# Starting the next stage inside the stage before it, at four seams of a one-core kernel

## What is computed

```python
x = x + L0_conv(_ln_c(x)); t = tokens(x); t = t + L0_ffn(_ln_t(t))   # 13x13 + 3x3 depthwise; experts
x = x + L1_conv(_ln_c(x)); t = tokens(x); t = t + L1_ffn(_ln_t(t))   # attention, 6 heads; experts
x = x + L2_conv(_ln_c(x)); t = tokens(x); t = t + L2_ffn(_ln_t(t))   # deformable attention; experts
x = x + L3_conv(_ln_c(x)); t = tokens(x); t = t + L3_ffn(_ln_t(t))   # linear attention; binarised layer

def _L1_ffn_ref(x, gate_w, gate_b, w1, b1, w2, b2):                  # the same for L0 and L2
    probs = softmax(einsum('bsd,de->bse', x, gate_w) + gate_b)       # 4 experts, the best 2 kept
    masked = probs * mask; masked = masked / (sum(masked) + 1e-09)
    h = gelu(einsum('bsd,edh->ebsh', x, w1) + b1)                    # 96 -> 384
    y = einsum('ebsh,ehd->ebsd', h, w2) + b2
    return einsum('bse,ebsd->bsd', masked, y)
```

## Time and profile before

| | |
|---|---|
| time, median of 3 runs | 1336.79 us (1335.22 to 1337.23) |
| the profiled execution | 1334.63 us, its span 1332.8 us |
| PE busy | 1177.9 us, 88% of the span |
| PE weight loads | 1020.5 us, 77% |
| DVE busy | 809.8 us, 61% |
| ACT busy | 487.3 us, 37% |
| POOL busy | 249.9 us, 19% |
| mean granted clock of TensorE | 0.929 of full speed |

### The profile page before, as it was taken

How to read it: one execution, slowest core, us unless ns; L and a number is a source line. 1 busy time by engine, 2 the same in 40 slices (tenths; PEclk the granted TensorE clock), 3 DMA queues, 4 the chain that set the end, 5 groups by cost and what they waited for, 6 DMA issues and landing times. The chain is left out here.

```text
span 1332.8 us, 23847 instructions
## 1 busy us (share of the span) xinstructions
PE 1177.9 (88%) x8368; PEld 1020.5 (77%) x8368; DVE 809.8 (61%) x2938; ACT 487.3 (37%) x948; POOL 249.9 (19%) x232
## 2 busy tenths in 40 slices
PE   2979999948999997999996999997999968998776
PEld 2978888937999996888894767676889867886455
DVE  6137676555666653767656665545767667776556
ACT  3524333314554543433331223224333322232542
POOL 3002212121010100221213343322121212111200
PEclk9989999967999998999996999997999988999577
DMA  3201010010000000000000000000000000000000
GB/s 136 76 24 49 14 47 0 0 48 1 1 2 1 2 1 1 1 1 0 0 1 0 1 1 2 1 1 1 1 1 0 0 1 1 1 1 1 3 10 36
DMA packets 11561, 15.67 MB, mean 12 GB/s; under 512 B 7385, under 2 KB 9007, under 8 KB 11346
## 3 DMA queue, kind: packets, MB, share of 16 engines
q1 hardware_dynamic: 10754, 12.86, 3.0%
q10 hardware_dynamic: 720, 1.66, 0.3%
HBM read 11.37 MB, written 3.15 MB: 11 GB/s over the span
## 5 line engine op out<-in xcount | busy, mean ns | idle before, releaser
L663 PEld LDWEIGHTS moe_dn<-all_w,moe_hid 128*128 128x128 f32 x2304 | 270.1, 192 | 5.9
L663 PE MATMUL moe_dn<-all_w,moe_hid 128*128 128x96 f32 x2304 | 271.5, 275 | 0.0
L600 ACT ACTIVATE moe_hid<-moe_up 128x512 f32<-128x512 f32 x288 | 169.7, 598 | 233.9 <-PE moe_up L655 221.8
L653 PE MATMUL moe_up<-moe_xh,moe_w1h 97*128 97x512 f32 x288 | 124.1, 431 | 0.0
L655 PE MATMUL moe_up<-moe_xl,moe_w1h 97*128 97x512 f32 x288 | 115.7, 402 | 0.0
L654 PE MATMUL moe_up<-moe_xh,moe_w1l 97*128 97x512 f32 x288 | 115.5, 401 | 0.0
L558 DVE SCALAR_TENSOR_TENSOR all_X<-moe_dn,moe_gate,all_X 128x96 f32 (+1 forms) x384 | 95.2, 310 | 33.4 <-PE moe_dn L663 29.1
L550 DVE SCALAR_TENSOR_TENSOR all_X<-all_b,moe_gate,all_X 128x96 f32 (+1 forms) x384 | 96.6, 314 | 10.8 <-DVE all_X L558 7.8
L481 POOL TENSOR_TENSOR moe_prob<-moe_euler,moe_logit 128x16 f32<-128x16 f32 x24 | 69.6, 2902 | 141.7 <-DVEq L517 141.7
L1060 PE MATMUL l1c_o<-l1c_vs,l1c_pt 128*128 128x64 f32 x768 | 94.4, 277 | 0.8 <-DVE l1c_ro L853 0.8
L1060 PEld LDWEIGHTS l1c_o<-l1c_vs,l1c_pt 128*128 128x128 f32 x768 | 91.8, 195 | 3.2 <-issue 1.4
(11 more groups left out here) (338 smaller groups left out, 2027.6 us busy)
## 6 DMA issues: line engine op xcount, KB each, us to landing
all_w<-w SPq DMA_DIRECT2D x3, 582.0 KB
all_w<-w SPq DMA_DIRECT2D x3, 576.0 KB
all_X<-x_rows SPq DMA_DIRECT2D x2, 768.0 KB, 6.7
conv_scratch<-all_X SPq DMA_DIRECT2D x2, 768.0 KB, 3.2
all_X<-conv_scratch SPq DMA_DIRECT2D x2, 768.0 KB, 4.7
out_tokens<-l3f_y SPq DMA_DIRECT2D x5, 288.0 KB, 2.1
l0c_band<-band ACTq DMA_DIRECT2D x1, 1248.0 KB, 9.2
all_b<-b SPq DMA_DIRECT2D x3, 192.0 KB
```

The source lines that it names most:

```text
L600: act.activation(hid[:, n, :], up[n % UPS][:, :], ACT.Gelu).then_inc(hid_done, 1)
L653: pe.matmul(bank, w1h[:, n, :], xh[:, p, :], start=True, stop=False)
L663: last = pe.matmul(dn[e % 2][:, j * C:(j + 1) * C], hid[:, n, j * P:(j + 1) * P], w2[:, n, :], start=(k == 0), stop=(k == KC - 1))
```

## The change

What a `moe` stage needs for its step 0 moves into a class `ExpertFront`, whose tiles live as long as the kernel. For layer 0 the same calls stand where they stood. For layers 1 and 2 they stand within `l1_attention` and `l2_conv`, in free parts of their banks. The first statistics, tokens and weights of `l2_conv` and `l3_conv` move into `ThirdFront` and `FourthFront`, called in the last step of the `moe` stage before (`follow`). `token_moments` is as in `l2_conv` before, over 8 tiles.

```diff
+class ExpertFront:
+    def pool_rstd(self, pool):
+        pool.wait_ge(self.var_done, 1)
+        pool.tensor_tensor(self.rstd[:, :], self.var[:, :], self.mhalf[:, :], ALU.pow).then_inc(self.rstd_done, 1)
+    def pool_exp(self, pool):
+        pool.wait_ge(self.logit_done, 1)
+        pool.tensor_tensor(self.prob[:, :, :], ..., self.logit[:, :, :], ALU.pow).then_inc(self.exp_done, 1)
...
+    def dve_gates(self, dve, chain):
+        dve.wait_ge(self.gates_in, 1)
+        choose_experts(dve, chain, self, self.gp.rearrange("p (t e) -> p t e", e=NE), 0, ...)   # was gates_of
...
+    def act_tokens(self, act):
+        act.wait_ge(self.turned, 1)
+        act.activation(self.xh[0:C, 0, :], self.tp[0:C, :], ACT.Copy)
+        act.activation(self.xt[0:C, 0, :], self.tp[0:C, :], ACT.Copy).then_inc(self.xt_done, 1)
...
+class ThirdFront:
+    def pool(self, pool):
+        pool.memset(self.mhalf[:, :], -0.5).then_inc(self.consts, 1)
+        pool.memset(self.xp[:, :, :, :], 0.0).then_inc(self.consts, 1)
+        pool.wait_ge(self.consts, 2)
+        pool.wait_ge(self.var_done, 1)
+        pool.tensor_tensor(self.rstd[:, 0:8], self.var[:, 0:8], self.mhalf[:, 0:8], ALU.pow
+                           ).then_inc(self.rstd_done, 1)
+        self.make_diag(pool, 1)
+        self.make_diag(pool, 0)
+    def dve_tokens(self, dve, chain):
+        dve.wait_ge(self.rstd_done, 1)
+        for t in range(4):
+            ins = dve.tensor_scalar(self.xn[:, 0, t, :], self.T["X"][:, t, :], ...)
+        ins.then_inc(self.xn_done, 1)
+    def pe_turn(self, pe):
+        pe.wait_ge(self.xn_done, 1)
+        for t in range(4):
+            ins = pe.transpose(self.tp[0:C, t * P:(t + 1) * P], self.xn[:, 0, t, :], self.T["ident"][:, :])
+        ins.then_inc(self.turned, 1)
...
+class FourthFront:
+    def dve_weights(self, dve, chain):
+        dve.wait_ge(self.bn_pow, 1)
+        chain.sync(dve.tensor_tensor(inv[:, :], inv[:, :], bn[:, 0, :], ALU.mult))
+        chain.sync(dve.tensor_tensor(shift[:, :], bn[:, 2, :], inv[:, :], ALU.mult))
+        dve.tensor_tensor(shift[:, :], bn[:, 1, :], shift[:, :], ALU.subtract).then_inc(self.folded, 1)
...
+    def pe_rest(self, pe):
+        pe.wait_ge(self.folded, 1)
+        pe.matmul(self.bank[0:C, 0:C], self.T["l3_wvt"][:, :], self.T["l3_wo"][:, :], start=True, stop=True)
+        pe.matmul(self.bank[:, C:C + 1], self.T["l3_wq"][:, :], self.shift[:, 0:1], start=True, stop=True
+                  ).then_inc(self.vw_in, 1)
@@ moe, vector engine, step (last step only)
                 bias_sums(g, p, chain)
+                if begun:
+                    begun.dve_sums(dve, ahead)
                 expert_sum(g, p, 0, chain)
+                if begun:
+                    begun.dve_tokens(dve, ahead)
                 expert_sum(g, p, 1, chain)
+                if begun:
+                    begun.dve_weights(dve, ahead)
                 expert_sum(g, p, 2, chain)
+                if begun:
+                    begun.dve_rest(dve, ahead)
                 expert_sum(g, p, 3, chain)
@@ moe, tensor engine, step
                     ups(g, p, e)
+                    if e == NE - 1 and last and follow:
...
+                        follow.pe_turn(pe)
+                        follow.pe_rest(pe)
                     downs(g, e - 1)
@@ moe, tensor engine, start
-            turn(0)
-            gates(0, 0)
-            pe.wait_ge(w_low, 1)
+            if layer == 0:
+                F.pe_turn(pe)
+                F.pe_gates(pe)
...
             ups(0, 0, 0)
@@ l1_attention, gpsimd: st == 5: F.pool_rstd, after the loop: F.pool_exp
@@ l1_attention, vector engine, end of iteration st
+                if st == 4:
+                    F.dve_stats(dve, chain)
+                if st == 6:
+                    F.dve_apply(dve, chain)
+                if 7 <= st < 7 + NE:
+                    F.dve_weights(dve, st - 7)
+                if st == NB - 2:
+                    F.dve_low(dve)
+                    F.dve_gates(dve, chain)
@@ l1_attention, scalar engine, end of iteration st
+                if 4 <= st < 4 + NE:
+                    F.act_weights(act, st - 4)
+                if st == NB - 2:
+                    F.act_tokens(act)
@@ l1_attention, tensor engine, ahead of values(st, 0)
+                if st == NB - 2:
+                    pe.wait_ge(S["unit_done"], 3 * NB)
+                    F.pe_turn(pe)
+                if st == NB - 1:
+                    F.pe_gates(pe)
@@ l2_conv, gpsimd
+                if p == 4:
+                    F.pool_rstd(pool)
                 for i in range(2):
                     keys(p, i)
                 for i in range(2):
                     bilinear(p, i)
+            F.pool_exp(pool)
@@ l2_conv, vector engine, end of iteration p
+                if p == 3:
+                    F.dve_stats(dve, chain)
+                if p == 4:
+                    F.dve_apply(dve, chain)
+                if 3 <= p < NP - 1:
+                    F.dve_weights(dve, p - 3)
+                if p == NP - 1:
+                    F.dve_low(dve)
+                    F.dve_gates(dve, chain)
@@ l2_conv, tensor engine: p == 7: F.pe_turn after turn_values(6), F.pe_gates ahead of positions(7)
```

More of the change, by code:

```diff
@@ L407, in moe @@
+def moe(nc, T, A, layer, follow=None):
     w1, w2, gw, b2 = T["moe"][layer]
-    X, ident = T["X"], T["ident"]
+    X, ident, F = T["X"], T["ident"], T["front"]
+    w1h, w1l, xn, xt, xh, xl, gate = F.w1h, F.w1l, F.xn, F.xt, F.xh, F.xl, F.gate
     STEPS = NT // GT
@@ L519, in gates_of @@
-                for e in range(NE):
-                    dve.memset(rank[:, :, e], float(NE - 1 - e))
-                wait(dve, exp_done, g + 1)
-                chain.sync(dve.tensor_reduce(smax[:, :], prob[:, :, :], AX.X, ALU.add))
-                chain.sync(dve.reciprocal(smax[:, :], smax[:, :]))
-                chain.sync(dve.tensor_tensor(prob[:, :, :], prob[:, :, :], wide(smax[:, :]), ALU.mult))
-                for d in range(1, NE):
-                    last = dve.tensor_tensor(ge[:, d - 1, :, 0:NE - d], prob[:, :, 0:NE - d], prob[:, :, d:NE],
-                                             ALU.is_ge)
@@ L540, in gates_of @@
[L540 to L543 removed]
+                wait(dve, gates_in, g)
+                choose_experts(dve, chain, F, scores.rearrange("p (t e) -> p t e", e=NE), p, logit_done, gates_read,
+                               exp_done, g)
@@ L564, in step @@
                 chain = Chain(dve, dve_step, base + g * EACH)
+                begun = follow if last else None
+                ahead = Chain(dve, follow.step) if begun else None
                 bias_sums(g, p, chain)
@@ L668, in step @@
                 for e in range(1, NE):
-                    if isinstance(g, int) and g == 0:
-                        wait(pe, w_low, e + 1)
+                    if layer == 0 and isinstance(g, int) and g == 0:
+                        wait(pe, F.w_low, e + 1)
                     ups(g, p, e)
@@ L1282, in normalise @@
             def normalise(p):
-                wait(dve, S["rstd_done"], next(n for n, (lo, hi) in enumerate(BATCHES) if 4 * p < hi) + 1)
+                wait(dve, S["rstd_done"], next(n for n, (lo, hi) in enumerate(BATCHES) if 4 * p < hi))
                 wait(dve, S["turned"], p - 1)
```

481 lines of the change are left out of this document (306 added, 175 removed).

## The result

The changed kernel takes 1328.28 us (median, 1327.45 to 1331.33) against 1336.79 before: ratio 0.9943, 95% interval [0.9931, 0.9955], 7.6 to 8.5 us less, where 12.4 were forecast. The profiled execution took 1329.28 us, its span 1327.5.

A forecast was written before the change was run, and what follows sets the result against it. PE sets the pace inside stages; time is lost at the seams, where PE idles behind serial chains. Terms -2.6 - 0.4 + 8.3 + 7.9 - 0.8 = 12.4 us saved, from 1336.79 to 1324.4 (range 1316.5 to 1331.5).

The forecast's parts named there:

- Seam 1: Attention to layer 1's experts: 8.15 us saved, but an 8.0 stall and 3.35 of low clock lost; sum -2.6.
- Seam 2: Third convolution to layer 2's experts: 8.15 and 3.15 us saved, 8.35 stall and 3.35 low clock lost; sum -0.4.
- Seam 3: Layer 1's experts to third convolution: 9.4 us saved, 1.6 from the clock, 2.7 lost waiting for tokens; sum +8.3.
- Pieces: Statistics, norms and weight parts within full stages fall mostly into engine waits; -0.8 us (0 to -4).
- Rival 2: Seams 1 and 2: the clock stays low through the rest of both stages; 16.2 us lost, 1340.6; chance 0.14.
- my case: Seam 2: the stage's rest is 11.6 us, longer than the low stretch of 7, so `ups` start at full clock.
- Rival 4: Seam 3: DVE comes first at the port shared with POOL, so the norms are not stretched; 1322.1; chance 0.07.
- Seam 4: Experts to last convolution: `conv_kv(0)` at 1087.9 instead of 1096.03, 1.4 us lost waiting for the folded shift; sum +7.9.
- Rival 1: Seams 1 and 2: the clock comes back soon, seam 1's `ups` start at full clock; 1318.7; chance 0.17.
- Rival 3: Full stages: the pieces are not covered, all 15 us push PE; 1338.6, slower; chance 0.03.
- Rival 5: Seams 1 and 2: no stalls, gates done beside other work, some 11 us more each; 1302; chance 0.02.
- Rival 6: Stage starts: nothing gained, as the new start waits for something unseen at the barrier; 1333 to 1338; chance 0.04.

The follow-up runs named there:

- e1: Changed kernel with the gates' chain on DVE in the attention behind `norm_heads(14)` instead of ahead of it; 1320.74 us, 0.9883.
- e5: Changed kernel plus 32 unread products of 512 columns on PE behind the attention's gate products, filling the stall; 1322.03 us, 0.9897.
- e8: e1 plus eight unread products of 512 columns on PE behind the attention's gate products; 1313.36 us, 0.9831.
- e10: e7 plus ten unread products of 512 columns on PE behind the last `downs` of each expert stage; 1303.01 us, 0.976.
- e4: Changed kernel with seams 1 and 2 undone: only the third and the last convolution are begun early; 1319.84 us, 0.9878.
- e3b: Changed kernel with POOL building the two diagonal weights after PE's token turn, not beside DVE's four norms; 1326.13 us, 0.9927.
- e2: Changed kernel with the part of the third convolution's gates' chain that needs POOL's exponential deferred to the start of layer 2's experts; 1322.67 us, 0.9896.
- e11: Changed kernel with gate products, exponential and gates' chain back at the start of the experts for layer 2 alone; 1322.03 us, 0.9901.
- e7: Changed kernel with gate products, exponential and gates' chain back at the start of the experts in layers 1 and 2; 1304.83 us, 0.9763.
- e12: e10 with five unread products instead of ten behind each expert stage's last `downs`; 1305.21 us, 0.9767.
- e3: Changed kernel with PE turning the third convolution's first tokens behind the `downs` of expert 2 instead of ahead of them; 1326.44 us, 0.9929.

## Why the prediction was right, and where its terms were wrong

**The time** (1328.28, forecast 1324.4 with 1316.5 to 1331.5) lies in the range, and each wait stands where the order of the streams put it. What was wrong by more than 1 us was the clock each time.

That the total is off by 3.9 only is partly luck. In the traces the gain is 5.3 and not 12.4: seams 1, 2 and 3 were 4.0, 2.3 and 3.2 too favourable, 9.5 together. The pieces gave back 0.8, and the last convolution 2.7 against 1.1 lost ahead of the attention, which no term had. The medians show 3.2 more than the traces. From `conv_kv(0)` on the instructions are the same in the changed kernel and in all twelve of the experiments, yet from there to the end are 234.1 us in the changed kernel, e1, e5 and e8, 236.3 to 237.4 in seven others, 232.7 in e10 and 231.8 in e4 (before: 236.8). So the 2.7 are no yield of the change.

**Seam 1, forecast -2.6, measured -6.6.** The saving (8.15), the stall (8.0; measured 519.19 - 509.43 - 1.58 = 8.18), the transposes (0.4; 0.48) and the first step's wait (1.0; 1.3) were right. The term that failed is "one more low stretch ... I take 7: 7 x 0.48 = 3.35". It measured 7.4 (21.46 from `values(15, 0)` to the first `ups`, against 523.07 + 0.4 - 509.43 = 14.04 before) and e5 says 7.2. The step behind it was to take the length of a low stretch from other places, as if it ended by itself. e1 and e8 show that it lasted here until PE got other work. And "PE is idle for some 7.5 us there", the reason given for it, is not needed: in e1 the clock fell without it. The comparison behind that reason, "longer than the idle stretches behind which the clock fell", was misread too: of those three PE's last wait in seam 3 was 10.03 us, and in seam 1 the clock had fallen at 519.9, 2.8 us ahead of the wait of 4.99.

**Rival 2** (the clock stays low through the rest of both stages) was the right mechanism for seam 1. It counted the rest as 8.1 us and its price as 4.8 beyond the sum; 4.1 came of it. The argument against it, that no low stretch in the rows is longer than 10.3, was a count of three. In seam 2 the stretch ended inside the stage, 11.2 us after PE took up work: there my case and not the rival's.

**Seam 2, forecast -0.4, measured -2.7.** Saving 8.15 (8.2), stall 8.35 (903.24 - 892.11 - 2.65 = 8.5) right. The low stretch cost 4.5 instead of 3.35 (the last addition ends at 919.70 instead of 904.08; 15.6 less 2.65 less 8.5), and of "the `ups` should start at the full clock" 2.1 of 3.15 came (920.02 to 935.73 against 912.63 to 930.41): they started at 1.00, and the clock fell at 921.3 for 3.4 us. About 0.4 of the 2.1 is a wait for tokens at 927.87 of before that went, and not the clock. The cause of the low stretch is less sure than its price, since one came in e4 in the same place without the stall.

**Seam 3, forecast +8.3, measured +5.1.** The wait (2.2; 2.04), its reason (3.70; 3.69, shown by e3b), the start behind the barrier (9.4; 718.48 - 716.64 instead of 714.38 - 703.44, 9.1) and the gain in the low stretch (1.6; 1.4) were right. Missing was the low clock over the 48 `downs`, 8.17 - 5.49 = 2.7 us, and over the transposes, 0.5. It was no part of the sum because I tied a fall to waits of 7 us. It is also not a fixed price: with the same wait of 2.04 the clock fell in the changed kernel, e1, e2, e5, e8 and e11 (the 48 `downs` took 6.81 to 8.22 us), and did not in e4, e7, e10 and e12 (5.50). Rival 4, DVE first at the port, did not come: POOL's row stands 0.07 us ahead.

**Seam 4, forecast +7.9, measured +7.9.** PE waits 0.27 for the folded shift where under 1 was forecast, `conv_kv(0)` starts 2.15 us behind the last addition.

**Pieces, forecast -0.8, measured 0.0** in both stages: DVE's and ACT's waits covered all of them.

Rivals 1, 3, 5 and 6 did not come. Rival 5 (the stalls are not there, 1302) prices rightly what the same idea gives with the gates done beside other work: e7 gives 1304.8.

**Still open** is what exactly makes the clock fall. Eight traces have the attention's gate products, with the same instructions on PE up to there. The clock fell within 0.2 us of their end in six of them (the changed kernel, e1, e2, e3, e3b, e8), 3.4 us behind it, in the idle stretch, in e11, and not at all in e5. Behind the same eight products in the third convolution (890.42) and in the loop (557.15) of the changed kernel it stayed at 1.00. So the products are neither shown to be the cause nor ruled out. The 1.1 us lost ahead of the attention and the 2.7 won behind `conv_kv(0)` go with low stretches of other lengths at places that the change hardly touches; no experiment was made on them.

## What to carry to other kernels

Move the part of a stage's start that has no chain behind it (tokens, statistics, weight parts) into the stage before, and leave the part that ends in a serial chain (here gate products, exponential, ranking) where work of its own stage covers it: this took 31.7 us, the whole move 7.6. Before putting a chain into an in-order stream, look at who is behind it on that engine. And price a stall on TensorE by what PE does afterwards, not by a typical length: in the changed kernel the clock came back 5.2 us into the `ups`, and not once in the 21.5 us of the attention's end ahead of them.

## What the runs showed of the hardware

- TensorE's granted clock fell from 2.4 to 1.2 GHz at 512.95 in e1 with PE busy for the whole of each window around it; the work ahead of it was eight products of 4 columns in 1.06 us. The attention's last images ran at 0.50 for the rest of the stage there, and at 1.00 until 521.5 in e7, with nearly the same rows.
- In e8 it came back at 514.5, at the end of eight products of 512 columns in 3.66 us, and stayed for 10 us.
- Behind a wait of 2.04 us it fell in six kernels and not in four. In e4 it fell at 886.7 behind a wait of 0.50, in the kernel before it did not.
- Two POOL rows of 1.6 us beside four DVE norms: 3.69 us for the norms, 1.05 without them.
